# Weight subtractions in pieces of 240 and 256 columns, attention values loaded ahead of weights, and a few steps in another order

## The chip, the cores and the metric

The kernel runs on one core of a Trainium2 chip. The metric is the device time of one execution in microseconds (us), as the median of the runs. Before the change it is 815.58 us, over three runs of 815.52 to 818.22.

The engines are named as in the profile: PE is TensorE, PEld its weight loads, DVE is VectorE, ACT is ScalarE, POOL is GpSimd, SP issues DMAs.

## The reference

Two transformer-like layers on `x` of shape (16, 128, 256). The first mixes with a long convolution and a mixture of experts, the second with causal attention of 16 heads and a LoRA mixture of experts:

```python
x = x + tanh(g_xattn[0]) * L0_xattn(layernorm(x), k, fside_S2_0, ctx, ctx, 8)   # convolution stage
x = x + tanh(g_ffn[0])   * L0_ffn(layernorm(x), Wr, Wg, Wu, Wd, Sg, Su, Sd, Wsg)
x = x + tanh(g_xattn[1]) * mha(layernorm(x), ctx, ctx)                           # attention
x = x + tanh(g_ffn[1])   * L1_ffn(layernorm(x), gate_w, w_up, w_gate, w_down, ...)

def mha(q, k, v):                     # 16 heads of 16 columns, 128 queries, 128 keys
    scores = einsum("bhqd,bhkd->bhqk", qh, kh) / sqrt(hd)
    scores = where(causal, scores, -10000.0)
    return einsum("bhqk,bhkd->bhqd", softmax(scores), vh)
```

Everything is float32. Matrix products of the two feed-forward parts are made from a high and a low part of each operand: the high part is a copy in TensorE's rounded float32 (`fp32r`), the low part is the original minus the high part.

## The kernel before

The program is written by hand, engine by engine, with semaphores: each engine has one in-order list of instructions, and where it stands in the code is where it runs. The work is done for G = 4 groups of four batch rows. Its stages follow one another, with the first steps of each beside the last of the one before:

- The convolution stage, up to about 165 us. For each group and each of 16 head steps DVE multiplies (`a_kv`, L1168), PE convolves, DVE multiplies again (`a_z`, L1179), and POOL adds halves and quarters (`a_add`: L620 of 256 columns, L625 of 128). Between these adds, POOL makes the low parts of the shared experts' weights, `split_low` (L611): six tiles, five of 768 columns and one of 512. The first two come before the adds, the others behind adds 5 and 10 of groups 0 and 1 (`SPLITS`). DVE waits for POOL's add of the step before (`zh_ready`), POOL for DVE's product (`z_ready`).
- The experts, up to about 391 us, at whose end rows are scattered and then gathered back into `X` by DMAs that POOL issues (`gather`, L670, eight for each group).
- Attention, about 391 to 559 us, 32 steps: g is the group, k = 0 to 7 the half batch row in it. For a step, PE makes scores (`c_scores`: L2122, with the mask L2126), DVE takes the row maximum (L1551), bounds it (L1555) and subtracts it (L1561, all `c_shift`), ACT exponentiates (L910), PE turns the result (L2136, `c_turn_p`), ACT copies it out (L919, `c_evac`), PE multiplies with the values (L2147, `c_values`), ACT copies (L930, `c_take_ot`), PE turns back (L2160) and every second step DVE divides and adds to `X` (`c_finish`: L1569, L1570, L1575). The queries of later steps are normalised beside this, by small DVE instructions (`c_norm`: L1089 to L1121, taken a few at a time between the others through the object `Steps`) and an ACT instruction (L772, `c_norm_one`), and turned by PE (L2167).
- The last feed-forward part, from about 559 us to the end. Its weights are loaded and split during attention: SP loads a tile of 960 columns (`weights1`, L531), ACT copies the high part (L905, `c_high`) at k = 1 and 5, and POOL subtracts (L704, `split_low1`, 8 tiles). It stands behind all 32 gathers in POOL's list, in a loop.

SP's loop of attention loads, for each half group r, the keys of the next group (16 DMAs, L521), then a weight tile, which waits until POOL has done with the tile before it (`w1L_ready`), then the values of the next group (L525), which wait until PE has used the old ones (`pv_done`):

```python
sp.wait_ge(scores_ready, 8 * g + 4 * r + 4)
keys(g + 1, r)
weights1(g + 1, r)
sp.wait_ge(pv_done, 1 + 8 * g + 4 * r + 4)
values(g + 1, r)
```

Of the kernel before, what the change touches and what calls it, by code (L numbers as in the profile page):

```python
# [17 lines left out]
F32 = mybir.dt.float32  # L18
# [75 lines left out]
REGS_PER_LOAD = 20  # L94
XB = 12
AHEAD = 8
NORM_AT = (2, 0, 0)
NORMS_IN = {2: (4, 5), 3: (6, 7, 8), 4: (9, 10), 5: (11, 12), 6: (13, 14, 15)}
KBD_PIECES = 4
# [43 lines left out]
def flamingo_kernel(nc, x, ctx_nat, ctx_half, ctx_t, ctx_one, filt, bias, gates, w0, wr, w1, gw, ramp_in, out):  # L143
    es = ExitStack()
    with es:
# [280 lines left out]
        def _(sp):  # L426
# [101 lines left out]
            def weights1(g, r):  # L528
                if not isinstance(g, int) or g > 0:
                    sp.wait_ge(w1L_ready, 2 * g + r - 1)  # L530
                sp.dma_start(stg1[r], w1[bass.ds(2 * g + r, 1)].rearrange("a p n -> (a p) n")  # L531
                             ).then_inc(stg1_loaded[r], 16)
# [8 lines left out]
            with sp.Fori(0, G - 1) as g:  # L541
                for r in range(2):

                    sp.wait_ge(scores_ready, 8 * g + 4 * r + 4)
                    keys(g + 1, r)
                    weights1(g + 1, r)
                    sp.wait_ge(pv_done, 1 + 8 * g + 4 * r + 4)
                    values(g + 1, r)
            def rows(n):
                sp.wait_ge(rows_ready, n + 1)  # L550
                sp.dma_start(rows_d[n], prow).then_inc(rows_stored, 16)
                sp.wait_ge(rows_stored, 16 * (n + 1))
                if n >= 2:
                    sp.wait_ge(w_sum, n - 1)
                sp.dma_start(rb[n % 2], rows_d[n].rearrange("q t -> (q t)").partition_broadcast(P)
                             ).then_inc(rows_loaded, 16)
# [15 lines left out]
        def _(pool):  # L572
# [35 lines left out]
            def split_low(n):  # L608
                w = W0T if n < SJ - 1 else NSH - (SJ - 1) * W0T
                pool.wait_ge(wH_ready, n + 1)  # L610
                nc.gpsimd.tensor_tensor(sL[:, n * W0T:n * W0T + w], stg[:, n % 2, 0:w],  # L611
                                        sH[:, n * W0T:n * W0T + w].bitcast(F32), ALU.subtract).then_inc(wL_ready, 1)

            def a_add(g, h):

# [70 lines left out]
            for i in range(4):  # L686
                pool.wait_ge(y_stored[i], 16 * ((NBLK - 1 - i) // 4 + 1))
            pool.wait_ge(y_slots_ready, 2)
            for g in range(G):
                if g == PRE and PRE < G - 1:  # L690
                    zero_keys()
                pool.wait_ge(b_done, 1 + 2 * (g + 1))
                for i in (0, 2):
                    gather(g * BG + i, 0)
                    gather(g * BG + i + 1, 0)
                    for k in (i, i + 1):
                        pool.wait_ge(gathered[0][k], 16 * (g + 1))
                        gather(g * BG + k, 1)

            def split_low1(g, r):  # L700
                n = 2 * g + r
                pool.wait_ge(w1H_ready, n + 1)
                dst = bass.ds(n * W1C, W1C)
                nc.gpsimd.tensor_tensor(w1L[:, dst], stg1[r], w1H[:, dst].bitcast(F32), ALU.subtract  # L704
                                        ).then_inc(w1L_ready, 1)
            with pool.Fori(0, G) as g:
                for r in range(2):
                    split_low1(g, r)
            pool.wait_ge(w1L_ready, W1K)
# [14 lines left out]
        def _(act):  # L724
# [251 lines left out]
            for b in range(2):  # L976
                nc.scalar.activation(qT[:, b], bank[2][:, b * D:(b + 1) * D].rearrange("p (k t) -> p k t", k=DT),
                                     ACT.Copy).then_inc(qT_ready, 1)
            c_exp(0, 0)
            c_norm_one(0, 2)  # L980
            c_exp(0, 1)
            c_evac(0, 0)
            for g in range(G - 1):
                c_steps(g, True)
            c_steps(G - 1, False)
# [92 lines left out]
        def _(dve):  # L1078
# [763 lines left out]

            nc.vector.memset(OT, 0.0).then_inc(ot_zeroed, 1)
            c_shift(0, 0)
            rows_complete(0, 2, 4)
            c_norm(2, 4).take_all()
            c_shift(0, 1)
            c_shift(0, 2)
            for g in range(G - 1):
                c_steps(g, True)  # L1850
            c_steps(G - 1, False)
# [21 lines left out]
        def _(pe):  # L1873
# [313 lines left out]
            def c_steps(g, more):  # L2187
                for k in range(8):
                    turned = q_turned_in(g, k)
                    if turned:  # L2190
                        pe.wait_ge(ot_taken, 8 * g + k)
                        c_turn_q(*turned)
                    if not more and k in TURN_AT:
                        pe.wait_ge(ot_taken, 8 * g + k)
                        d_turn_x0(TURN_AT.index(k))
                    if k and (k < 6 or more):
                        c_scores(g + (k + 2) // 8, (k + 2) % 8)
                    if k:
                        c_turn_o(g, k - 1)
                    if turned:  # L2200
                        pe.wait_ge(qT_ready, BG * turned[0] + turned[1] + 1)
                    if not more and k in TURN_AT:
                        pe.wait_ge(x0T_ready, TURN_AT.index(k) + 1)
                    c_values(g, k)
                    if k < 7 or more:
                        c_turn_p(g + (k + 1) // 8, (k + 1) % 8)
                if more:
                    c_scores(g + 1, 2)
                c_turn_o(g, 7)
# [267 lines left out]
```

## Time and profile before

| | us |
|---|---|
| median of 3 runs (lowest, highest) | 815.58 (815.52, 818.22) |
| the profiled execution | 818.64 |
| its span, from the first instruction to the last | 816.9 |
| PE busy | 697.7 (85%) |
| DVE busy | 581.1 (71%) |
| ACT busy | 308.1 (38%) |
| POOL busy | 234.1 (29%) |

Mean granted TensorE clock over the span: 0.929, where 1 is 2.4 GHz and 0.5 is 1.2 GHz. In the chain that ended last PE has 56%, DVE 19% and POOL 6% of the span. A busy share is an average over stages with different limits; what matters is what is waited for in the stage in question. A row of a timeline reads: start, duration, engine, line, operation, output<-input, shape, count, and in brackets the idle time of the engine before it with what ended it. A DVE or POOL duration begins when the engine takes the instruction up, so time in which it cannot reach its operands is inside the duration.

### The profile page before, as it was taken

The page shows a single profiled execution, that of the slowest core. Times are in us where ns is not written, and L with a number is a line of the kernel's source. Part 1 is how long each engine was busy: PE and PEld are TensorE (multiplying, and loading weights), DVE is VectorE, ACT ScalarE, POOL GpSimd, SP SyncE. Part 2 cuts the span into 40 slices and gives each one's busy share as a digit, 9 for nine tenths or more (in the row PEclk, how much of TensorE's full clock was granted, in tenths as well). Part 3 has the DMA queues.
Part 4 walks back from the last instruction along what each step waited for, and adds up shares of the span by engine and source line. Part 5 has one row for each costly group of instructions (what it writes and reads, how often), then busy time and mean ns, then how long its engine had stood idle before and what let it go on. Part 6 is the DMA issues. An engine that isn't in the chain of part 4 may idle for free.

```text
span 816.9 us, 12649 instructions
## 1 busy us (share of the span) xinstructions
PE 697.7 (85%) x4198; PEld 563.6 (69%) x4214; DVE 581.1 (71%) x1234; ACT 308.1 (38%) x542; POOL 234.1 (29%) x246
## 2 busy tenths in 40 slices
PE   2878889889887799998787898877698999999994
PEld 1556667678776799987555565545587888888883
DVE  5888898675774466755679797874488768768664
ACT  2201101047632344423266575744344344343330
POOL 1888787710377000007675111101000000000000
PEclk9999999999999799999689796968799999999996
DMA  8202100033223344415553221100101001010000
GB/s 286 87 15 71 39 14 14 1 103 91 93 100 140 102 119 121 120 49 95 117 84 79 72 78 48 52 1 1 52 1 52 1 27 53 19 34 27 26 0 26
DMA packets 42925, 51.30 MB, mean 63 GB/s; under 512 B 7088, under 2 KB 36976, under 8 KB 42224
## 3 DMA queue, kind: packets, MB, share of 16 engines
q1 hardware_dynamic: 36720, 41.98, 16.5%
q0 software_dynamic: 6144, 8.52, 5.1%
q8 instruction: 36, 0.59, 0.3%
q14 instruction: 25, 0.20, 0.1%
HBM read 36.88 MB, written 13.59 MB: 62 GB/s over the span
## 4 chain that ended last, share of the span: by engine, by line
PE 56%; DVE 19%; issue 7%; POOL 6%; ACT 6%; SPq 4%; DMA 3%; DVEq 0%; POOLq 0%; ACTq 0%
PE bank L2216 22%; PE bank L2065 5%; PE bank L2085 4%; PE bank L2001 4%; PE bank L2136 3%; POOL A L620 2%; PE bank L2122 2%; DVE A L1561 2%; PE bank L2015 2%; DVE small L1551 2%; POOL A L625 2%; PE bank L1909 1%; POOL R L611 1%; PE bank L1921 1%; PE bank L2147 1%
## 5 line engine op out<-in xcount | busy, mean ns | idle before, releaser
L2216 PE MATMUL bank<-R 128*128 128x512 f32 (+3 forms) x1080 | 221.9, 366 | 21.5 <-DVE A L1684 6.1
L2216 PEld LDWEIGHTS bank<-R 128*128 128x128 f32 (+1 forms) x1080 | 183.5, 193 | 57.2 <-issue 7.3
L670 POOL DMA_INDIRECT X<-y_d,A x32 | 50.1, 1564 | 123.3 <-DMA y_d<-A 105.3
L2001 PE MATMUL bank<-R 128*128 128x512 f32 x264 | 67.4, 407 | 0.9 <-DVE R L1519 0.9
L620 POOL TENSOR_TENSOR A<-A 128x256 f32<-128x256 f32 x64 | 58.8, 918 | 7.6 <-DVE A L1179 7.5
L1909 PE MATMUL bank<-A 128*128 128x256 f32 x128 | 42.5, 414 | 19.8 <-DVE A L1168 7.1
L2001 PEld LDWEIGHTS bank<-R 128*128 128x128 f32 x264 | 50.4, 197 | 11.2 <-DVE R L1519 1.2
L1551 DVE TENSOR_REDUCE small<-bank 128x8 f32<-128x1024 f32 x32 | 38.9, 1217 | 26.1 <-PE bank L2126 26.0
L1179 DVE TENSOR_TENSOR A<-bank,A 128x512 f32<-128x512 f32 x64 | 43.8, 685 | 17.0 <-PE bank L1911 13.5
L720 POOL TENSOR_TENSOR A<-A 128x512 f32<-128x512 f32 x4 | 5.1, 1287 | 176.2 <-DVE A L1669 176.2
L1168 DVE TENSOR_TENSOR A<-A 128x512 f32<-128x512 f32 x64 | 53.0, 829 | 2.1 <-ACT A L746 2.1
L1700 DVE TENSOR_TENSOR A<-bank,A 128x512 f32<-128x512 f32 (+1 forms) x48 | 33.0, 688 | 28.0 <-PE bank L2216 27.6
L664 POOL DMA_INDIRECT x_d<-A x32 | 35.6, 1111 | 58.5 <-DVE A L1347 49.1
L2065 PE MATMUL bank<-R 128*128 x234 | 49.9, 351 | 0.7 <-DVE R L1507 0.7
L2015 PE MATMUL bank<-R 128*128 128x256 f32 (+1 forms) x288 | 42.2, 299 | 9.0 <-DVE R L1437 8.9
L2136 PE MATMUL bank<-ident,A 128*128 128x128 f32 x256 | 42.3, 319 | 7.5 <-ACT A L910 7.5
L1016 ACT ACTIVATE A<-bank 128x512 f32<-128x512 f32 (+1 forms) x48 | 28.6, 595 | 52.7 <-PE bank L2216 52.6
L2015 PEld LDWEIGHTS bank<-R 128*128 128x128 f32 (+1 forms) x288 | 39.5, 203 | 12.9 <-DVE R L1437 6.8
L704 POOL TENSOR_TENSOR R<-A,R 128x960 f32 x8 | 18.4, 2381 | 102.9 <-ACT R L905 102.9
L1909 PEld LDWEIGHTS bank<-A 128*128 128x128 f32 x128 | 20.6, 193 | 38.4 <-issue 37.5
L625 POOL TENSOR_TENSOR A<-A 128x128 f32<-128x128 f32 x64 | 42.8, 669 | 14.1 <-PE bank L1921 9.3
L2136 PEld LDWEIGHTS bank<-ident,A 128*128 128x128 f32 x256 | 33.7, 164 | 16.5 <-issue 8.6
(246 smaller groups left out, 1348.6 us busy)
## 6 DMA issues: line engine op xcount, KB each, us to landing
A<-x_d SPq DMA_DIRECT2D x39, 132.0 KB, 2.2
y_d<-A SPq DMA_DIRECT2D x39, 128.0 KB, 1.7
A<-rows_d SPq DMA_DIRECT2D x4, 1024.0 KB, 4.8
A<-in_w SPq DMA_DIRECT2D x8, 480.0 KB, 3.7
A<-in_w SPq DMA_DIRECT2D x5, 512.0 KB, 3.8
A<-in_ctx_one SPq DMA_DIRECT2D x8, 272.0 KB, 3.7
A<-in_ctx_half SPq DMA_DIRECT2D x8, 256.0 KB, 2.6
A<-in_ctx_nat SPq DMA_DIRECT2D x4, 512.0 KB, 3.9
```

The costliest lines, as they stand in the source:

```text
L620: nc.gpsimd.tensor_tensor(zh[:, u], zr[:, u, :, 0:HALF, :], zr[:, u, :, HALF:, :], ALU.add).then_inc(zh_ready, 1)
L625: nc.gpsimd.tensor_tensor(z2[:, :, :, h * I0:(h + 1) * I0], zh[:, u, :, 0:QUARTER, :], zh[:, u, :, QUARTER:, :], ALU.add).then_inc(z2_read ...
L670: nc.gpsimd.indirect_dma_start(out=X[:, b], out_offset=None, in_=y_d[:, :], in_offset=bass.IndirectOffsetOnAxis(ap=y_slots[:, b, r:r + 1], ...
L1168: nc.vector.tensor_tensor(kv[:, u], vT[:, :, t0:t0 + I0].unsqueeze(3).to_broadcast([P, 8, I0, I0]), c.unsqueeze(2).to_broadcast([P, 8, I0, ...
L1179: nc.vector.tensor_tensor(zr[:, u], yb[u].rearrange("p (q i j) -> p q i j", q=8, i=I0), c.unsqueeze(3).to_broadcast([P, 8, I0, I0]), ALU.m ...
L1551: step.mark(nc.vector.tensor_reduce(mx[:, u], S, AX_X, ALU.max))
L1909: nc.tensor.matmul(y[:, 0:n], diag, kv0, start=True, stop=False, skip_group_check=True)
L2001: mm = nc.tensor.matmul(dst, wX[:, a0:a0 + P], mX[:, k], start=(m == 0), stop=(m == 5))
L2015: mm = nc.tensor.matmul(DN[:, b * D:(b + 1) * D], hX[0:pr, n % 2, b * P:(b + 1) * P], wX[0:pr, a0:a0 + D], start=(j == 0 and m == 0 and b ...
L2065: mm = nc.tensor.matmul(GU[i % 2][:, 0:2 * EF], xX[:, i % 2, k * P:(k + 1) * P], w[:, k, :, :, bass.ds(expert[i] * RANK, RANK)], start=(m ...
L2136: mm = nc.tensor.transpose(PTP[:, h * P:(h + 1) * P], E_[:, k % 2, h], ident[:])
L2216: mm = nc.tensor.matmul(dst, a, m, start=start and n == 0, stop=stop and n == len(prods) - 1, skip_group_check=skip)
```

## The change

- `split_low` issues each subtraction as pieces of D = 256 columns (three, for the last tile two), `split_low1` as four pieces of W1Q = 240 columns. The semaphore is raised by the last piece.
- The first two of the eight `split_low1` no longer stand behind all gathers: the first stands ahead of the gathers of group 2, the second ahead of those of group 3. The loop over the rest is written out.
- SP's loop loads the values ahead of the weight tile.
- At the start of attention, DVE makes the second shift ahead of the normalisation of rows 2 and 3, and ACT copies out the first turned tile and makes the second exponential ahead of the normalised row.
- In the last group, PE makes scores (3, 6) and (3, 7) ahead of turning the rows of the next stage (`d_turn_x0`).

```diff
+W1Q = 240
@@ SP, the loop of attention
                     keys(g + 1, r)
-                    weights1(g + 1, r)
                     sp.wait_ge(pv_done, 1 + 8 * g + 4 * r + 4)
                     values(g + 1, r)
+                    weights1(g + 1, r)
@@ POOL, split_low
-                nc.gpsimd.tensor_tensor(sL[:, n * W0T:n * W0T + w], stg[:, n % 2, 0:w],
-                                        sH[:, n * W0T:n * W0T + w].bitcast(F32), ALU.subtract).then_inc(wL_ready, 1)
+                for q in range(0, w, D):
+                    at = n * W0T + q
+                    part = nc.gpsimd.tensor_tensor(sL[:, at:at + D], stg[:, n % 2, q:q + D],
+                                                   sH[:, at:at + D].bitcast(F32), ALU.subtract)
+                part.then_inc(wL_ready, 1)
@@ POOL, gathers and split_low1
+            def split_low1(g, r):
+                n = 2 * g + r
+                pool.wait_ge(w1H_ready, n + 1)
+                for q in range(0, W1C, W1Q):
+                    part = nc.gpsimd.tensor_tensor(w1L[:, n * W1C + q:n * W1C + q + W1Q], stg1[r][:, q:q + W1Q],
+                                                   w1H[:, n * W1C + q:n * W1C + q + W1Q].bitcast(F32), ALU.subtract)
+                part.then_inc(w1L_ready, 1)
+
             for g in range(G):
                 if g == PRE and PRE < G - 1:
                     zero_keys()
+                if g >= 2:
+                    split_low1(0, g - 2)
                 pool.wait_ge(b_done, 1 + 2 * (g + 1))
...
-            with pool.Fori(0, G) as g:
+            for g in range(1, G):
                 for r in range(2):
                     split_low1(g, r)
@@ ACT, start of attention
             c_exp(0, 0)
+            c_evac(0, 0)
+            c_exp(0, 1)
             c_norm_one(0, 2)
-            c_exp(0, 1)
-            c_evac(0, 0)
@@ DVE, start of attention
             c_shift(0, 0)
+            c_shift(0, 1)
             rows_complete(0, 2, 4)
-            c_norm(2, 4).take_all()
-            c_shift(0, 1)
-            c_shift(0, 2)
+            norm = c_norm(2, 4)
+            norm.take(4)
+            c_shift(0, 2, norm)
+            norm.take_all()
@@ PE, c_steps
+                    if k and (k < 6 or more):
+                        c_scores(g + (k + 2) // 8, (k + 2) % 8)
                     if not more and k in TURN_AT:
                         pe.wait_ge(ot_taken, 8 * g + k)
                         d_turn_x0(TURN_AT.index(k))
-                    if k and (k < 6 or more):
-                        c_scores(g + (k + 2) // 8, (k + 2) % 8)
```

Where instructions move, the lists read as follows. First ACT at the start of attention, before: A is the buffer of exponentials, turned tiles and rows, bank is PSUM, small the turned output.

```order
L910 ACTIVATE A<-A 128x1024 [waits shifted]
L772 ACTIVATE A<-X,A 128x256 [waits ln_ready]
L910 ACTIVATE A<-A 128x1024 [waits shifted]
L919 ACTIVATE A<-bank 128x1024 [waits p_turned]
L930 ACTIVATE small<-bank 128x256 [waits pv_done]
```

The same place after it, where the line numbers are those of the changed file (L918 is the exponential, L927 the copy of the turned tile, L780 the normalised row, L938 `c_take_ot`):

```order
L918 ACTIVATE A<-A 128x1024 [waits shifted]
L927 ACTIVATE A<-bank 128x1024 [waits p_turned]
L918 ACTIVATE A<-A 128x1024 [waits shifted]
L780 ACTIVATE A<-X,A 128x256 [waits ln_ready]
L938 ACTIVATE small<-bank 128x256 [waits pv_done]
```

The normalised row now stands directly ahead of `c_take_ot`, and behind the copy and the second exponential.

POOL's list after the change, at the gathers of group 2 (L674) and the first two subtractions in pieces (L697; A and y_d are the gather's slots and source, R the split weights):

```order
L674 DMA X<-y_d,A 128x256 [waits gathered0_3]
L697 TENSOR_TENSOR R<-A,R 128x240 [waits w1H_ready]
L697 TENSOR_TENSOR R<-A,R 128x240 x3
L674 DMA X<-y_d,A 128x256 [waits b_done]
L674 DMA X<-y_d,A 128x256
```

Before, every gather came first and the loop of subtractions behind them:

```order
L670 DMA X<-y_d,A 128x256 [waits gathered0_2]
L670 DMA X<-y_d,A 128x256 [waits gathered0_3]
L706 UNCONDITIONAL_BRANCH
L706 ISA
L704 ISA [waits w1H_ready]
L704 TENSOR_TENSOR R<-A,R 128x960
L702 REGISTER_ALU
L704 ISA [waits w1H_ready]
L704 TENSOR_TENSOR R<-A,R 128x960
```

So the gathers of groups 2 and 3 are now behind a wait for ACT's copy of a weight tile.

## Rows read from the trace of the kernel before

**Rows 1.** Stretches: us; busy PE, PEld, DVE, ACT, POOL; granted clock; DMA share, GB/s.

```profile
396.00:414.00 18.00, 13.22 (x76) 8.73 (x78) 11.35 (x29) 6.64 (x9) 11.17 (x8) 0.54 0.49 98
...
445.00:458.40 13.40, 12.02 (x65) 7.96 (x70) 8.04 (x20) 7.39 (x11) 0.40 (x1) 0.51 0.25 78
...
458.40:493.00 34.60, 30.55 (x320) 20.66 (x318) 32.08 (x66) 24.57 (x36) 4.74 (x3) 0.99 0.22 63
...
493.00:506.40 13.40, 11.73 (x70) 7.16 (x70) 8.83 (x19) 5.60 (x10) 1.54 (x1) 0.50 0.24 69
...
533.00:546.70 13.70, 9.21 (x59) 5.64 (x60) 9.39 (x23) 5.16 (x8) 0.00 (x0) 0.54 0.00 0
```

**Rows 2.** DVE's timeline at 437 us, and line 704 there.

```profile
437.52 4.45 DVE L1575 TENSOR_TENSOR X<-X,A 128x256 f32<-128x256 f32 x1
...
L704 POOL TENSOR_TENSOR R<-A,R x2: 2794/2804/2815, 436.7 to 438.9; 128x960 f32 x2
```

**Rows 3.** Timeline of SP, then PE, 411 to 444 us.

```profile
411.92 13.01 SPq L521 DMA_DIRECT2D A<-in_ctx_t  x16
...
439.68 0.35 SPq L531 DMA_DIRECT2D A<-in_w  x1
...
440.33 0.40 SPq L525 DMA_DIRECT2D A<-in_ctx_one  x1
...
443.87 0.65 PE L2147 MATMUL bank<-A 128*17 128x128 f32 x16 [2.00 <-DMA A<-in_ctx_one]
```

**Rows 4.** DVE's timeline, four maxima.

```profile
444.49 1.21 DVE L1551 TENSOR_REDUCE small<-bank 128x8 f32<-128x1024 f32 x1
...
457.82 1.23 DVE L1551 TENSOR_REDUCE small<-bank 128x8 f32<-128x1024 f32 x1 [3.32 <-PE bank L2126]
...
481.88 1.23 DVE L1551 TENSOR_REDUCE small<-bank 128x8 f32<-128x1024 f32 x1 [0.51 <-PE bank L2126]
...
489.89 1.22 DVE L1551 TENSOR_REDUCE small<-bank 128x8 f32<-128x1024 f32 x1
```

**Rows 5.** Lines 620, 1168: ns min/median/max, first and last start; then POOL's timeline.

```profile
L620 POOL TENSOR_TENSOR A<-A x64: 712/728/1700, 26.5 to 157.1; 128x256 f32<-128x256 f32 x64
...
L1168 DVE TENSOR_TENSOR A<-A x64: 650/683/1776, 17.3 to 153.5; 128x512 f32<-128x512 f32 x64
...
72.62 1.81 POOL L611 TENSOR_TENSOR R<-A,R 128x768 fp32r<-128x768 f32 x1
```

**Rows 6.** Start of attention: timeline of DVE, ACT and PE.

```profile
396.86 0.74 DVE L1089 BATCH_NORM_STATS2 A<-X 128x6 f32<-128x256 f32 x2
...
400.49 0.16 DVE L1121 SCALAR_TENSOR_TENSOR A<-A 128x2 f32<-128x2 f32 x1
...
403.17 1.21 DVE L1551 TENSOR_REDUCE small<-bank 128x8 f32<-128x1024 f32 x1
...
400.69 0.60 ACT L772 ACTIVATE A<-X,A 128x256 f32<-128x256 f32 x1 [2.66 <-DVE A L1121]
...
405.36 1.07 PE L2147 MATMUL bank<-A 128*17 128x128 f32 x16 [2.27 <-issue]
...
408.12 0.63 PE L2167 MATMUL bank<-ident,A 128*128 128x128 f32 x2
```

**Rows 7.** ACT's and POOL's timeline, 405 to 422 us.

```profile
417.26 0.99 ACT L905 ACTIVATE R<-A 128x960 fp32r<-128x960 f32 x1
...
405.91 1.54 POOL L670 DMA_INDIRECT X<-y_d,A  x1 [0.30 <-issue]
...
421.39 1.54 POOL L670 DMA_INDIRECT X<-y_d,A  x1 [0.30 <-issue]
```

**Rows 8.** DVE's timeline at two later subtractions.

```profile
459.08 1.17 DVE L1102 TENSOR_SCALAR A<-A 128x4 int32<-128x4 int32 x1
...
530.70 2.19 DVE L1114 TENSOR_TENSOR A<-A 128x4 f32<-128x4 f32 x1
```

**Rows 9.** PE's timeline in the last group.

```profile
541.05 0.66 PE L2173 MATMUL bank<-ident,A 128*128 128x128 f32 x2 [1.69 <-ACT A L941]
```

More of the change, by code:

```diff
@@ L698, in _ @@
                         gather(g * BG + k, 1)
[L700 to L705, printed above, removed]
-            with pool.Fori(0, G) as g:
+            for g in range(1, G):
                 for r in range(2):
```

## The prediction

> **What bounds the kernel now.** I read the stretches first, then the chain of waits, then the timelines of the places that the change touches. Attention runs from 391 to 559 us, some 168 us for 32 steps. The reader is to see in the stretches [rows 1] that PE is busy 88% of 458.4 to 493 at a granted clock of 0.99, and that the clock is at half (1.2 GHz, 0.50 to 0.54) in four stretches of 13 to 18 us. In three of them PE is as busy as elsewhere, so there PE's half speed is the bound; ahead of each PE had stood still for part of some us. At full speed DVE is as full as PE (32.1 against 30.6 of 34.6 us). So a stall of DVE can cost twice: by itself, and by the clock that falls behind it.
>
> The largest stall is at 437 us [rows 2]: DVE's addition to X (L1575), 0.42 us elsewhere, takes 4.45 us. POOL runs two subtractions of 960 columns there, 2.8 us each, from 436.7 to 441.7, and DVE is let in only at their end. Behind it PE waits another 2.0 us, to 443.87, for values that SP issued at 440.33, because they stood behind a weight tile that waited for POOL until 439.68; the keys ahead of both were out by 424.9 [rows 3]. Then the clock is at half.
>
> The rows for this say two things of the change. DVE waits for a whole POOL instruction, which speaks for short ones. But the second subtraction starts at 438.9, before the first has ended (436.7 + 2.8 = 439.5), and DVE does not get in between. The Trainium skill (GPSIMD Engine Reference, 2.1 Instruction dispatch) says that the cores of GpSimd begin their share of the next instruction without waiting for each other; the overlap of these two agrees, and by that rule adjoining pieces could hold DVE out as one long instruction. It is rival B below. In the convolution stage the same DVE operation never takes more than 1.78 us [rows 5] beside adjoining POOL instructions, so there it does get in.
>
> **The change, part by part.** Times are against the profiled execution, 818.64 us (span 816.9); that is 3.06 above the median of 815.58.
>
> 1. *Pieces of 256 in the convolution stage.* POOL's add of 256 columns takes 0.71 us undisturbed, a whole subtraction of 768 columns 1.81 [rows 5]. Three pieces with some 0.04 of overlap at each joint are 2.05, so +0.24 for each of five tiles, and about +0.1 for the one of two pieces: 1.3 us. POOL runs without a gap through most of groups 0 and 1 and DVE waits for its adds, so nothing hides it. DVE's L1168 (0.65 undisturbed, 1.78 at most, [rows 5]) would be held 1.1 us less for each tile: at best 6 × 1.1 = 6.6 less; at worst DVE comes in at one joint more of each tile, 6 × 0.65 = 3.9 more. It is POOL that is late, so I stay near its own row: **+1.3** (-2 to +4; all 6.6 would need POOL to have slack).
>
> 2. *Start of attention.* PE now gets its first turned tile at 401 instead of 405.3, as ACT no longer waits for the normalised row, and the 2.27 us of idle PE ahead of L2147 go [rows 6]. But the normalisation, 19 small steps from 396.86 to 400.65, is now broken up: 4 steps ahead of the third maximum, 4 beside it, 11 behind it. That maximum waits for scores and still starts at 403.17. Maximum, four small steps of 0.2 and subtraction are 3.2 us, to 406.4, and eleven steps of 0.2 end at 408.5. ACT's normalised row, 0.60 long and begun at 400.69 before, then ends at 409.2. `c_take_ot` stands behind it on ACT (0.4 us), and PE's turn of the query waits for both: 409.6 instead of 408.12 [rows 6], so +1.5. PE idles from about 406 to 409.6 at half clock, and the return to full clock may come later. Work at half clock costs double, so I add 0.4: **+1.9**. Bounds: -2.3 if nothing is late behind the idle time that goes, +4 if the clock returns some us later.
>
> 3. *First two subtractions ahead of gathers.* The first now follows ACT's copy (417.26 + 0.99, [rows 7], and about 2 later by part 2): 420.5 to 423, beside a normalisation on DVE. Up to one piece of 0.7 us is waited for at once: **+0.7**, bounds 0 and 2.7 (all four pieces). The gathers of group 2 follow, eight in 421.39 - 405.91 = 15.5 us [rows 7], so to 438.6 and landed by some 442.5. DVE wants them at about 448, so they are hidden by 5 us. Those of group 3 have 20 us and more.
>
> 4. *The pair at 437 us.* The two subtractions are now 16 us apart and in pieces. DVE's next maximum starts when the scores are there, at 441.7 instead of 444.49 [rows 4]; the values are in by 430, as they are issued right behind the keys. That is -2.8 on DVE, -3.2 on PE: **-3.0**. Without the values ahead of the weights, PE would still have stood until 443.8, and about 1.2 would be left; so of the 3.0 some 1.8 hang on that edit. Bounds: -0.5 if the pieces hold like one instruction, and -4.
>
> 5. *The clock behind it.* From 444.49 to 457.82 are two steps, 13.3 us at half clock; from 481.88 to 489.89 two steps with a normalisation too, 8.0 us at full clock [rows 4]. So 5.3 us if the fall at 445 goes. But full clock fell in the same part of the next group (493) and in the last (533) [rows 1], and not in that of group 0. I take half: **-2.7**, bounds 0 and -5.3.
>
> 6. *Later subtractions.* At 459.08 a small DVE step takes 1.17 instead of 0.17 us, at 530.70 one takes 2.19 instead of 0.16 [rows 8]. In pieces of 0.65 the first such step waits less. But it stands in a row of small steps 0.2 apart, and each of these finds the next piece: about as many waits as pieces, 0.5 each, sum 2. A gain is only there where a long DVE instruction on PSUM follows. **-0.3**, bounds -3 and +2.
>
> 7. *Scores ahead of turned rows.* PE's wait of 1.69 us for ACT's normalised row [rows 9] goes, as the scores stood behind it and need nothing of it. In the next step the exponential waits about 0.4 longer for ACT's copy: **-1.3**, bounds -2 and 0.
>
> Sum: 1.3 + 1.9 + 0.7 - 3.0 - 2.7 - 0.3 - 1.3 = -3.4, so 815.2 in that execution, and 812.2 as the median.
>
> A rule of the Trainium skill bears on parts 1 and 6 (SBUF — State Buffer, SBUF: two separate sides, on the port pair that DVE and GpSimd share): whoever starts first has the pair for the whole instruction. The 4.45 us agree in kind. By it alone a piece would bound every wait at 0.7 us, and part 6 would be -3.0 instead of -0.3.
>
> **The rivals.**
>
> A. *The clock stays up.* If stalls are shorter, the falls at 445 and at 493 or 533 may both go: 2.7 more in part 5, and for the other, of 0 to 5.3 by the same rows, I take 3.3. 812.2 - 2.7 - 3.3 = 806.2. For it: those stretches each follow a DVE stall on POOL. Against: at 493 the clock fell before the stall there could have slowed PE.
>
> B. *Pieces hold as one.* Parts 3 and 4 go to 2.7 and -1.5, part 6 to +0.7: 812.2 + 2.0 + 1.5 + 1.0 = 816.7. For it: the overlap in [rows 2]. Against: L1168's maximum [rows 5].
>
> C. *The start of attention costs and nothing is given back*, the case on the other side. The place is ACT's wait for the normalised row, ahead of `c_take_ot`. Part 2 goes to +4, and the later time shifts the steps so that the clock falls once more, in the one normalisation that ran at full clock (group 0, 415 to 431): +5.3, with part 5 at 0. 812.2 + 2.1 + 5.3 + 2.7 = 822.3. It decides once ACT's row ends later than about 409 and PE idles over 3 us there. For it: a fall behind PE's idle time at 396 [rows 1]. Against: stretches of a normalisation did pass at full clock.
>
> **How the numbers follow.** Forecast (809 to 816): 0.45. A: 0.25. B: 0.15. C: 0.15. A measurement of this kernel tells 0.5% from no change, which is 4.1 us: faster is below 811.5, slower above 819.7. The forecast's own range gives 0.19 faster and 0.26 same; A 0.23 and 0.02; B 0.01 and 0.11 with 0.03 slower; C 0.03 same and 0.12 slower. Together 0.43 faster, 0.42 same, 0.15 slower. The range for 8 in 10 takes in most of A, all of B and a part of C: 804 to 820.
>
> **What would show it.** Part 1: the last step of group 1 in the convolution stage about 1 us later, and DVE's L1168 never over 1.4. Part 2: PE's first turn of a query near 409.6 + 1.3, with over 3 us of idle PE ahead of it. Part 4: no L1575 over 1.2 us, no PE wait for values. Part 5: full clock through 445 to 458. Part 6: several DVE steps of 0.5 to 0.8 us in place of one of 2. Part 7: no PE wait for ACT's L941 ahead of scores. Wrong would be: an L1575 of 2 us or more (B), a DVE wait for gathered rows in group 1, or a new stretch at half clock between 415 and 437 (C).

## The result and the profile after

The changed kernel takes 806.62 us (805.19 to 815.86, 13 runs), the kernel before 818.22 beside it; the ratio is 0.988, 95% interval [0.9845, 0.9915]. In two later comparisons on other chips it was 0.991 [0.9874, 0.9946] and 0.9908 [0.9875, 0.9941]. So it is faster by about 1%, some 7 to 10 us, where 3.4 were forecast. The profiled execution of after took 805.39 us (span 803.6, mean granted clock 0.949), that of before 818.64 (816.9 and 0.929): 13.25 less. It is one of the changed kernel's quicker executions, so the ledger below, which is of this pair, adds up to more than the medians differ by.

The ledger goes by the starts of DVE's maxima (L1551 before, L1559 after), one for each of the 32 steps of attention; (g,k) is step k of group g. Eight of them as DVE's timeline of after has them (start us, duration us, then the operation and the idle time ahead):

```profile
394.11 1.16 DVE L1559 TENSOR_REDUCE small<-bank 128x8 f32<-128x1024 f32 x1
412.83 1.23 DVE L1559 TENSOR_REDUCE small<-bank 128x8 f32<-128x1024 f32 x1 [4.65 <-PE bank L2136]
435.10 1.22 DVE L1559 TENSOR_REDUCE small<-bank 128x8 f32<-128x1024 f32 x1 [0.73 <-PE bank L2136]
442.66 1.23 DVE L1559 TENSOR_REDUCE small<-bank 128x8 f32<-128x1024 f32 x1 [0.17 <-PE bank L2136]
450.79 1.22 DVE L1559 TENSOR_REDUCE small<-bank 128x8 f32<-128x1024 f32 x1
482.47 1.22 DVE L1559 TENSOR_REDUCE small<-bank 128x8 f32<-128x1024 f32 x1
498.59 1.22 DVE L1559 TENSOR_REDUCE small<-bank 128x8 f32<-128x1024 f32 x1
536.50 1.23 DVE L1559 TENSOR_REDUCE small<-bank 128x8 f32<-128x1024 f32 x1
```

| step | before | after | after less before | gained since the row above |
|---|---|---|---|---|
| (0,0) | 394.29 | 394.11 | -0.18 | -0.18 |
| (1,0) | 434.12 | 435.10 | +0.98 | +1.16 |
| (1,2) | 444.49 | 442.66 | -1.83 | -2.81 |
| (1,4) | 457.82 | 450.79 | -7.03 | -5.20 |
| (2,4) | 489.89 | 482.47 | -7.42 | -0.39 |
| (2,7) | 508.90 | 498.59 | -10.31 | -2.89 |
| (3,5) | 536.03 | 525.33 | -10.70 | -0.39 |
| (3,7) | 549.75 | 536.50 | -13.25 | -2.55 |

All of the difference has arisen by the last step of attention. The convolution stage gave nothing in the end, the start of attention cost 1.2 us, the place at 437 us gave 2.8, and the two steps behind it 5.2. The gain from (2,4) to (2,7) is not in every execution: another profile of the changed kernel (c2_after) takes 18.70 us for these three steps, where this one takes 16.12 and before takes 19.01.

The stretches say why these two steps shrank so much. First the stretches of [rows 1] in after, then after's own three at half clock in this part (busy PE, PEld, DVE, ACT, POOL; granted clock; DMA share, GB/s):

```profile
396.00:414.00 18.00, 12.35 (x71) 7.58 (x72) 10.08 (x27) 6.02 (x8) 4.53 (x3) 0.54 0.33 71
445.00:458.40 13.40, 11.54 (x116) 7.54 (x118) 12.84 (x37) 9.56 (x14) 8.79 (x6) 1.00 0.61 125
458.40:493.00 34.60, 29.23 (x288) 19.63 (x290) 31.22 (x62) 23.32 (x36) 8.77 (x13) 0.95 0.28 75
489.70:493.10 3.40, 3.40 (x28) 2.54 (x26) 2.58 (x4) 0.67 (x2) 0.00 (x0) 0.50 0.30 83
493.00:506.40 13.40, 12.73 (x125) 8.53 (x126) 10.24 (x15) 12.03 (x19) 2.30 (x4) 1.00 0.17 54
523.80:534.00 10.20, 8.85 (x58) 5.61 (x59) 8.29 (x22) 5.07 (x8) 0.00 (x0) 0.50 0.00 0
```

From 445 to 458.4 the clock was 0.51 before and is 1.00 now; PE issues 116 matmuls in place of 65 in about the same busy time. From 493 to 506.4, where it was 0.50, 3.4 us at half clock are left (489.7 to 493.1).

At 437 us the addition to X, 4.45 us in [rows 2], takes 0.87. DVE's timeline, then POOL's:

```profile
438.50 0.87 DVE L1583 TENSOR_TENSOR X<-X,A 128x256 f32<-128x256 f32 x1
439.29 1.21 DVE L1559 TENSOR_REDUCE small<-bank 128x8 f32<-128x1024 f32 x1
440.54 0.69 DVE L1563 TENSOR_SCALAR small<-small 128x8 f32<-128x8 f32 x1
...
436.74 1.54 POOL L674 DMA_INDIRECT X<-y_d,A  x1 [0.90 <-DMA X<-y_d,A]
437.73 3.46 POOL L697 TENSOR_TENSOR R<-A,R 128x240 fp32r<-128x240 f32 x4
```

SP's timeline answers to [rows 3]. The values (L526) and the weight tile (L532) are out by 426.7, ahead of the keys of 431, and nothing on SP waits for POOL. PE has no wait for a transfer in attention any more.

```profile
412.98 12.16 SPq L522 DMA_DIRECT2D A<-in_ctx_t  x16
425.43 0.41 SPq L526 DMA_DIRECT2D A<-in_ctx_one  x1
426.13 0.56 SPq L532 DMA_DIRECT2D A<-in_w  x1
431.11 11.95 SPq L522 DMA_DIRECT2D A<-in_ctx_t  x16
```

### The profile page after: what moved, and what is told of

Read it like the earlier page. It is cut to its first block, busy times and chain, and to the rows that moved or that the text cites. A ratio compares the mean times of both kernels' runs of the same rounds, so it can differ in the third digit from the quotient of the medians.

```text
span 803.6 us, 12659 instructions
## 1 busy us (share of the span) xinstructions
PE 685.7 (85%) x4198; PEld 555.2 (69%) x4214; DVE 575.7 (72%) x1234; ACT 307.8 (38%) x542; POOL 239.3 (30%) x281
## 4 chain that ended last, share of the span: by engine, by line
PE 55%; DVE 20%; issue 7%; POOL 6%; ACT 6%; SPq 4%; DMA 3%; DVEq 0%; POOLq 0%; ACTq 0%
PE bank L2226 23%; PE bank L2075 5%; PE bank L2095 4%; PE bank L2011 4%; DVE A L1569 2%; PE bank L2025 2%; POOL A L624 2%; PE bank L2146 2%; DVE small L1559 2%; PE bank L2132 2%; POOL R L614 2%; POOL A L629 2%; PE bank L1919 1%; PE bank L1931 1%; DVE A L1097 1%
## 5 line engine op out<-in xcount | busy, mean ns | idle before, releaser
L674 POOL DMA_INDIRECT X<-y_d,A x32 | 50.2, 1568 | 124.8 <-DMA y_d<-A 105.3
L624 POOL TENSOR_TENSOR A<-A 128x256 f32<-128x256 f32 x64 | 56.3, 880 | 7.6 <-DVE A L1187 7.5
L1176 DVE TENSOR_TENSOR A<-A 128x512 f32<-128x512 f32 x64 | 51.2, 801 | 2.1 <-ACT A L754 2.1
L1559 DVE TENSOR_REDUCE small<-bank 128x8 f32<-128x1024 f32 x32 | 38.9, 1216 | 17.4 <-PE bank L2136 17.3
L697 POOL TENSOR_TENSOR R<-A,R 128x240 fp32r<-128x240 f32 x32 | 22.9, 868 | 85.2 <-ACT R L913 85.2
L2146 PE MATMUL bank<-ident,A 128*128 128x128 f32 x256 | 38.9, 300 | 7.4 <-ACT A L918 7.2
L2146 PEld LDWEIGHTS bank<-ident,A 128*128 128x128 f32 x256 | 30.7, 153 | 15.9 <-issue 8.7
```

What stands on the lines that cost most here:

```text
L624: nc.gpsimd.tensor_tensor(zh[:, u], zr[:, u, :, 0:HALF, :], zr[:, u, :, HALF:, :], ALU.add).then_inc(zh_ready, 1)
L674: nc.gpsimd.indirect_dma_start(out=X[:, b], out_offset=None, in_=y_d[:, :], in_offset=bass.IndirectOffsetOnAxis(ap=y_slots[:, b, r:r + 1], ...
L1176: nc.vector.tensor_tensor(kv[:, u], vT[:, :, t0:t0 + I0].unsqueeze(3).to_broadcast([P, 8, I0, I0]), c.unsqueeze(2).to_broadcast([P, 8, I0, ...
L1559: step.mark(nc.vector.tensor_reduce(mx[:, u], S, AX_X, ALU.max))
L2146: mm = nc.tensor.transpose(PTP[:, h * P:(h + 1) * P], E_[:, k % 2, h], ident[:])
```

## The experiments

Each ran beside the kernel before. Steps are compared within profiles, totals by medians and intervals. There were three comparisons on three chips: one with e1 to e4, one with e5, e7, e8 and c_after, one with e6, e9, e10 and c2_after. The last two have the changed kernel itself as a control (812.75 and 810.54 us); the first has none, and there e4_weights_first (805.86 us), whose profile matches the changed kernel's, comes nearest to one. Line numbers of the runs differ from the changed kernel's by a few lines. Each fence of code shows the edit against the changed kernel, cut to the lines that change.

### Pieces taken back in attention (e3_attn_whole)

```
-W1Q = 240
+W1Q = 960
```

> The changed kernel with the eight subtractions of attention whole (960 columns), each still at its new place. Theory (the place pays, pieces hardly): the addition to X at 438 us waits up to 2 us once, the small DVE steps wait about as much in all; the total within 2 us of the changed kernel unless the clock falls once more (then 5 more). Rival (pieces are what pays): 5 us or more slower, with falls of the clock at 445 and 530 us as in the kernel before.

817.37 us (812.22 to 823.34), ratio 0.9987 [0.9956, 1.0018]: the whole gain is gone. Yet the place alone did repair 437 us: there the addition takes 0.97. The stall turned up 16 us later, at the second subtraction of the group (DVE's timeline and POOL's, then the stretch behind it):

```profile
458.58 3.33 DVE L1122 TENSOR_TENSOR A<-A 128x4 f32<-128x4 f32 x1
...
458.10 1.54 POOL L674 DMA_INDIRECT X<-y_d,A  x1 [0.30 <-issue]
459.07 2.81 POOL L697 TENSOR_TENSOR R<-A,R 128x960 fp32r<-128x960 f32 x1
```

```profile
458.40:472.00 13.60, 11.68 (x72) 6.85 (x69) 10.42 (x18) 4.42 (x7) 3.48 (x2) 0.51 0.37 87
```

A step on 4 columns, 0.16 us elsewhere, takes 3.33: it began inside the gather and ended with the subtraction (459.07 + 2.81 = 461.88). Then the clock is at 0.51. So moving whole subtractions moves the stall and the fall of the clock with it. From (1,4) to (2,0), the four steps around this stall, this kernel takes 22.51 us and the changed one 16.10. The theory that the place pays and the pieces hardly do fell.

### Place taken back, pieces kept (e5_pair)

```
-                if g >= 2:
-                    split_low1(0, g - 2)
...
-            for g in range(1, G):
+            for g in range(G):
```

> The changed kernel with all eight subtractions of attention behind the gathers again, but in pieces of 240. Theory (pieces alone take most of the stall, as DVE gets in between two of them; the place is secondary): eight pieces in a row near 437 us, the addition to X waits at most 1.2 us, the weight tile comes late but the values do not wait for it; the total within 2 us of the changed kernel. Rival (the place pays): DVE's steps beside eight pieces wait several us in all, the clock falls at 445 us, the total 5 us or more higher.

816.46 us (from 812.03; one of its 12 executions took 3652 us and weighs nothing in a median), ratio 0.9955 [0.9928, 0.9983]. DVE's timeline, then SP's, then PE's:

```profile
443.22 2.17 DVE L1581 TENSOR_TENSOR X<-X,A 128x256 f32<-128x256 f32 x1
...
431.30 0.41 SPq L526 DMA_DIRECT2D A<-in_ctx_one  x1
443.24 0.35 SPq L532 DMA_DIRECT2D A<-in_w  x1
443.85 12.19 SPq L522 DMA_DIRECT2D A<-in_ctx_t  x16
...
457.51 2.08 PE L2130 MATMUL bank<-A 32*128 32x256 f32 x8 [3.64 <-issue]
```

Here the eight pieces stand in a row behind the last gather, which runs from 438.86 to 440.40 (POOL's timeline):

```profile
439.85 6.07 POOL L697 TENSOR_TENSOR R<-A,R 128x240 fp32r<-128x240 f32 x8
```

The addition takes 2.17 us, half of [rows 2]: it is held over more than one piece, but let in at 445.39, before the last of them ends (445.92). From (1,0) to (1,2) it is 8.18 us, against 10.37 before and 7.56 in after, so at this place pieces alone bring most of the gain. But the weight tile still waits for POOL until 443.24, and now the next keys stand behind it: they go out at 443.85 instead of 431.11, the last is issued at 456.04, PE stands still for 3.64 us until 457.51, ahead of the first scores that use them, and step (1,4) starts 7.95 us behind (1,3) instead of 3.27. (The profile names no releaser for this wait; that it is the keys follows from SP's order and these times.) With values ahead of weights the hold has moved from the values to the keys. So in this order of SP's loads, pieces without the place are worth little, and both are needed. Pieces alone with the old order of the loads were not tried; there the values would again stand behind the late weight tile, as in [rows 3].

### Halves (e9_halves)

```
-W1Q = 240
+W1Q = 480
```

> The changed kernel with pieces of 480 columns in attention (1.35 us each) instead of 240. If DVE waits for at most the piece that is running, the addition to X at 437 to 441 takes at most some 1.8 us (0.42 + 1.35), the clock stays up behind it, and the total is 0 to 2 us above the changed kernel's. If the size must be small because adjoining pieces hold DVE out together, the addition or the subtraction beside them takes 2.5 us or more, the clock falls at about 455, and the total is 5 us or more above.

815.33 us (812.62 to 820.19), ratio 0.9967 [0.994, 0.9994], against 0.9908 for quarters beside it and 0.9987 for wholes in another comparison. The additions to X were never over 1.12 us, as the theory of the single piece has it. But at 458 us:

```profile
458.13 3.33 DVE L1124 SCALAR_TENSOR_TENSOR A<-A 128x4 f32<-128x4 f32 x1
...
457.51 1.54 POOL L674 DMA_INDIRECT X<-y_d,A  x1 [0.30 <-issue]
458.50 2.93 POOL L697 TENSOR_TENSOR R<-A,R 128x480 fp32r<-128x480 f32 x2
```

DVE's step began while the gather was open, 0.37 us ahead of the listed start of the subtraction, and was let go at the end of the second half (461.46 against 461.43): a hold as long as that of one whole. The gather alone does not hold such a step: in after one takes 0.16 at 456.91, inside the gather of 455.46 to 457.15. The clock was 0.75 from 458.4 to 472. Away from gathers there was no such long hold. The same small step behind the maximum of (0,4) meets the first subtraction in all three sizes (DVE's timelines of after, of halves, of wholes):

```profile
418.97 0.65 DVE L1563 TENSOR_SCALAR small<-small 128x8 f32<-128x8 f32 x1
```

```profile
420.56 1.17 DVE L1563 TENSOR_SCALAR small<-small 128x8 f32<-128x8 f32 x1
```

```profile
421.21 2.18 DVE L1563 TENSOR_SCALAR small<-small 128x8 f32<-128x8 f32 x1
```

0.65, 1.17, 2.18 for pieces of 0.69, 1.20, 2.22 us: there the wait is at most the piece that runs. The difference between the two places is in POOL's durations (ns min/median/max of L697, in after and in the kernel with wholes):

```profile
L697 POOL TENSOR_TENSOR R<-A,R x32: 684/695/1522, 418.9 to 544.9; 128x240 fp32r<-128x240 f32 x32
```

```profile
L697 POOL TENSOR_TENSOR R<-A,R x8: 2209/2220/2807, 421.1 to 556.0; 128x960 fp32r<-128x960 f32 x8
```

Behind a gather a subtraction starts 0.55 us before the gather is over (457.51 + 1.54 = 459.05 against 458.50) and is listed some 0.6 us longer, 2.81 for 2.22. Pieces behind it overlap by as much: there is no moment between them at which POOL has nothing open. The pair of the kernel before stood in the same way behind its last gather, which is open until 437.26 while the first subtraction is listed from 436.70 (POOL's timeline of before; for the pair see [rows 2]):

```profile
435.72 1.54 POOL L670 DMA_INDIRECT X<-y_d,A  x1 [0.88 <-DMA X<-y_d,A]
```

This overlap as the cause of the long holds is argued from the times, not shown by an experiment: no kernel kept a subtraction away from every gather. A skew between POOL's cores would fit what the Trainium skill says (Perfetto Trace Analysis, DMA Instruction — SWDGE (GPSIMD)): two of them write a gather's descriptors. No row here shows single cores.

### The changed kernel again (c2_after, c_after)

> The changed kernel itself, for comparison in this call: 805 to 813 us as in its earlier runs, ratio 0.985 to 0.994.

810.54 us, ratio 0.9908. Its profiled execution took 812.46, 7.1 more than that of after, and shows where one program's executions part. At (1,4) they are 0.23 us apart (451.02 against 450.79); then, behind the gathers (DVE, then the stretch):

```profile
457.57 1.74 DVE L1124 SCALAR_TENSOR_TENSOR A<-A 128x4 f32<-128x4 f32 x1
```

```profile
458.40:472.00 13.60, 11.29 (x86) 7.17 (x86) 9.32 (x18) 6.49 (x10) 0.89 (x2) 0.75 0.22 68
```

In after, DVE met the same four pieces with 0.37 and 0.62 (458.80 and 459.20) and the clock stayed up. By (2,0) the two are 4.9 us apart, and another 2.6 come between (2,5) and (2,7), where the clock is 0.62 from 493 to 506.4. So even quarters hold DVE together now and then when they overlap; its addition at 438.71 took 1.67 as well, over the 1.2 us that the prediction set as its mark. A hold of 1.7 need not cost that: e6_old_tail below had one of 1.73 at 460.7 and no fall before 494.9. What decides whether a hold is followed by a fall is not shown.

The other control:

> The changed kernel itself, as the mark for the other kernels of this call. Both theories: 805 to 808 us in most runs, 811 to 816 in some, and the same order of events as in its first profile.

812.75 us (804.85 to 816.35); its profiled execution (804.85) is after's within 0.5 us at nearly every maximum.

### Weights ahead of values (e4_weights_first)

```
                     keys(g + 1, r)
+                    weights1(g + 1, r)
...
                     values(g + 1, r)
-                    weights1(g + 1, r)
```

> The changed kernel with SP loading the weight tile ahead of the values again. Theory: POOL frees the tile at about 421 us, ahead of the end of the keys' issues, so the wait for it is short now and the values come only about 0.5 us later: no wait of PE for values, same total. Rival (the order of the loads is what pays): PE waits 2 us for values near 440 us and the total is 2 us or more higher.

805.86 us (805.1 to 813.73), ratio 0.9864 [0.9819, 0.9909], maxima equal to after's within 0.25 us. SP's timeline:

```profile
425.67 0.44 SPq L532 DMA_DIRECT2D A<-in_w  x1
426.40 0.40 SPq L526 DMA_DIRECT2D A<-in_ctx_one  x1
```

The tile's slot is free by then, because the first subtraction now comes ahead of the gathers. Beside the new place of the subtractions, the order of the loads is worth nothing.

### The tail's old order (e6_old_tail)

```
-                    if k and (k < 6 or more):
-                        c_scores(g + (k + 2) // 8, (k + 2) % 8)
                     if not more and k in TURN_AT:
                         pe.wait_ge(ot_taken, 8 * g + k)
                         d_turn_x0(TURN_AT.index(k))
+                    if k and (k < 6 or more):
+                        c_scores(g + (k + 2) // 8, (k + 2) % 8)
```

> The changed kernel with PE's turned rows again ahead of its scores in the last group; all else as changed. If part 7 of the prediction is right, PE again stands still some 1.7 us ahead of L2177's turned rows for ACT's normalised row, and the maxima of steps (3,6) and (3,7) come 1.3 to 2.3 us later than 531.67 and 536.50, so the total is 1.3 to 2.3 us above the changed kernel's of the same call. If the order of the tail is worth nothing because PE is at half clock there anyway or ACT's exponentials bound the steps, those maxima stay within 0.5 us and the total within 0.5.

813.15 us (808.57 to 818.97), ratio 0.9931 [0.9897, 0.9965]; 2.6 above the control, with intervals that overlap. The profile is clear: PE's wait is back, and (3,6) starts 8.69 us behind (3,5), as before, instead of 6.34 (PE, then DVE's two maxima):

```profile
535.31 0.66 PE L2183 MATMUL bank<-ident,A 128*128 128x128 f32 x2 [1.69 <-ACT A L949]
...
530.29 1.22 DVE L1559 TENSOR_REDUCE small<-bank 128x8 f32<-128x1024 f32 x1
538.98 1.22 DVE L1559 TENSOR_REDUCE small<-bank 128x8 f32<-128x1024 f32 x1 [4.03 <-PE bank L2136]
```

So the edit is worth 2.35 us in the profile: the wait of 1.69 and the turn itself, 0.66, which also stood ahead of the scores.

### The convolution stage's pieces taken back (e1_conv_whole)

```
-                for q in range(0, w, D):
+                for q in range(0, w, w):
```

(and slices of `w` for those of `D`)

> The changed kernel with the subtractions of the convolution stage whole again (768 columns). Theory (pieces there cost POOL time, about 0.24 us each tile): DVE's additions to X at the ends of groups 0 and 1 come 1.1 and 1.3 us earlier than in the changed kernel (at 65.9 and 101.7 us), the total 0 to 1.3 us lower if nothing later takes it back. Rival (pieces let DVE in and pay there): these additions come later than in the changed kernel, the total higher. Rival (the 1.3 us are given back by TensorE's clock behind 158 us): same total, with the half-clock stretch at 158.5 us back.

808.01 us (805.77 to 818.49), ratio 0.9854 [0.9814, 0.9894]: no worse than the changed kernel. The additions at the ends of groups 0 and 1 were expected at 65.9 and 101.7; they came at 67.93 and 103.78. This execution had already lost time early, with the clock at 0.79 from 26 to 34 us, where it is at 1.00 in after, so its profile can't be compared with after's by absolute times. From the one addition to the other it takes 35.85 us, before 35.84 and after 36.04.

In after, groups 0 to 2 end later than before: their last additions (L1202 before, L1210 after) are at 66.99, 103.03 and 136.49 against 65.85, 101.69 and 135.16, so +1.14, +1.34, +1.33. But the fourth is at 162.22 against 162.37. The stretch from 157 to 162 us, of before and of after:

```profile
157.00:162.00 5.00, 3.21 (x15) 3.21 (x16) 2.25 (x4) 0.00 (x0) 3.41 (x4) 0.66 0.02 5
```

```profile
157.00:162.00 5.00, 2.21 (x18) 1.87 (x17) 3.17 (x6) 0.00 (x0) 4.66 (x6) 1.00 0.02 5
```

Before, a part of it was at half clock; after, none. That gives the 1.3 us back. A kernel with whole subtractions in a quick execution (e10_best_again, below) confirms it: its additions are at 65.56, 101.42, 134.88 and 162.12, and its stretch is that of before:

```profile
157.00:162.00 5.00, 3.48 (x17) 3.49 (x18) 2.01 (x3) 0.00 (x0) 3.13 (x3) 0.66 0.02 5
```

That the clock would give it back is not something I could have read from before.

### The start of attention (e2_old_start, e7_mixed_start)

The first has the old order on both engines. The second has DVE's old order, and on ACT only the evacuation ahead:

```
             c_exp(0, 0)
             c_evac(0, 0)
-            c_exp(0, 1)
             c_norm_one(0, 2)
+            c_exp(0, 1)
...
             c_shift(0, 0)
-            c_shift(0, 1)
             rows_complete(0, 2, 4)
-            norm = c_norm(2, 4)
-            norm.take(4)
-            c_shift(0, 2, norm)
-            norm.take_all()
+            c_norm(2, 4).take_all()
+            c_shift(0, 1)
+            c_shift(0, 2)
```

> The changed kernel with the old order at the start of attention on DVE and ACT. Theory (the new order there costs, as the query's turn waits for the normalised row): PE's first turn of a query at 408.1 instead of 409.1 us, the maximum of step (0,3) about 1 us earlier, the total 0 to 1.5 us lower. Rival (the new start pays): the total 1 us or more higher.

> The changed kernel with DVE's old order at the start of attention (normalisation ahead of the second shift) and ACT copying the first turned tile ahead of the normalised row, then the second exponential. Theory (the start costs because DVE's normalisation ends late): the normalised row is ready at 401.3 us, PE's first turn of a query moves from 409.1 to about 406.5, the maximum of step (0,3) from 18.7 us behind that of step (0,0) to about 16; the total 1 to 3 us lower unless the clock's falls move. Rival (PE at half clock is the bound there, whatever the order): no change at step (0,3).

From (0,0) to (0,3) it is 17.48 us before, 18.72 after, 17.52 with the old start and 15.67 with the mixed one. The totals don't follow: 811.04 (ratio 0.9912 [0.9878, 0.9946]) and 810.79 (0.9881 [0.985, 0.9912]). In the mixed one's profile the clock was at half again at 465 us and for 10 us from 492.6, and what the start had saved was gone by (2,7): from (0,0) to there it takes 107.77 us, the changed kernel 104.48. So by itself the start shows in its own steps and not in the total.

### The best version (e8_best, e10_best_again)

The mixed start, and whole subtractions in the convolution stage.

> As the kernel with the mixed start, and the subtractions of the convolution stage whole. Theory: both gains, 1 to 3 us at the start of attention and 1.3 us in the convolution stage, so 2 to 4 us below the changed kernel if the clock's falls stay where they are. Rival (the clock decides): the total anywhere within 5 us of the changed kernel, following the mean granted clock.

> The same kernel as e8_best (convolution subtractions whole, DVE's old order at the start of attention, ACT: both first exponential and evacuation ahead of the normalised row, the second exponential behind it), beside the changed kernel in one call. If it is the better version, its ratio to before is again below 0.987 and its fastest runs lie 2 us or more below the changed kernel's (804 to 805). If the first result was luck of the clock, the two agree within 1 us in their fastest runs.

805.69 us (800.89 to 812.54), ratio 0.9844 [0.9797, 0.9891], and 806.55 (801.55 to 812.9), ratio 0.9878 [0.9833, 0.9924]; the second misses the expected 0.987 by a little. The changed kernel beside them: 812.75 and 810.54. Each pair of intervals overlaps. Taken together, the median of its 12 executions is 806.2, that of the changed kernel's 16 is 812.3, and five of the 12 lie below the lowest of the 16 (804.85). None of the changed kernel's 13 executions in the first comparison lies below 804.85 either, but their median is 806.62. So the quickest executions speak for this version; that its median is lower is not settled. DVE's third and fourth maxima show the start: the third comes at once (in after it stands behind 2.71 us of idle DVE), and the fourth comes 15.54 us behind the first (at 395.92 in this execution).

```profile
404.83 1.21 DVE L1559 TENSOR_REDUCE small<-bank 128x8 f32<-128x1024 f32 x1
411.46 1.23 DVE L1559 TENSOR_REDUCE small<-bank 128x8 f32<-128x1024 f32 x1 [3.95 <-PE bank L2134]
```

## Why the prediction was right and where it was not

The direction, the largest place and the terms 2, 4 and 6 held; the forecast of 812.2 us was 5.6 above the 806.6 measured, within its range. The gain was two to three times the 3.4 forecast. That the later medians of the changed kernel, 812.75 and 810.54, lie so near 812.2 is luck: the kernel before ran at 818.95 and 818.89 beside them, some 3.3 us above the 815.58 from which the forecast was taken.

One reading was wrong from the start. PE is not as busy as elsewhere in three of the four stretches at half clock [rows 1] but in two, 90% and 88%; in the other two it is 73% and 67%. So half speed bounds the two at 445 and 493, and the other two less.

1. *Convolution stage, +1.3.* The first three groups end 1.1 to 1.3 us later, and DVE's L1176 is never over 1.21 us, as said. What was missed is that the delay is given back at 157 to 162 us by the clock. Net -0.2.
2. *Start of attention, +1.9.* +1.16 by (1,0), +1.24 by (0,3). PE's turn of the query starts at 409.13 (409.6 forecast), behind 3.26 us of idle PE:

```profile
409.13 0.69 PE L2177 MATMUL bank<-ident,A 128*128 128x128 f32 x2 [3.26 <-ACT small L938]
...
408.21 0.60 ACT L780 ACTIVATE A<-X,A 128x256 f32<-128x256 f32 x1 [6.20 <-DVE A L1129]
408.71 0.36 ACT L938 ACTIVATE small<-bank 128x256 f32<-128x256 f32 x1
```

   The mechanism is the one named: the row on ACT waits 6.2 us for DVE's broken-up normalisation. ACT's small copy runs beside the row's end, which I had put behind it; that is the half microsecond. The 0.4 for the clock did not come. The order without that flaw is the mixed start, which is 3.05 us quicker to (0,3).
3. *First subtraction ahead of gathers, +0.7.* One small step waits 0.65, as said, but on DVE it costs the path nothing: (0,5) is +1.06, (1,0) +0.98. Gathers start 0.3 us later than before [rows 7] and nothing waits for them.
4. *The pair at 437, -3.0.* -2.81. Right in size. Wrong is that 1.8 of it hang on the values being loaded first: without that edit the step is the same (e4_weights_first). I had let the weight tile wait for POOL until 439.68 as before, though the subtraction it waits for had itself moved ahead of the gathers.
5. *The clock behind it, -2.7.* This is the term that was mis-sized. The whole 5.3 of its own working came (-5.20), and in all three profiles of the changed kernel the clock is at 1.00 from 445 to 458.4. Halving the term on the ground that the clock also falls at the same part of the next group was wrong: the fall at 445 went all the same. The fall at 493 shrank too in this pair, another -2.89, but not in every execution: from (2,4) to (2,7) after and c_after take 16.12 us, c2_after 18.70, before 19.01. Why it shrinks in some is not shown.
6. *Later subtractions, -0.3.* Small, as said (-0.39 from (1,4) to (2,4), and again from (2,7) to (3,5)), and the reason given is seen. DVE's row of small steps at 485 us meets one piece after the other:

```profile
485.62 0.49 DVE L1124 SCALAR_TENSOR_TENSOR A<-A 128x4 f32<-128x4 f32 x1
486.15 0.62 DVE L1119 SCALAR_TENSOR_TENSOR A<-A 128x4 f32<-128x4 f32 x1
486.81 0.61 DVE L1122 TENSOR_TENSOR A<-A 128x4 f32<-128x4 f32 x1
```

   1.24 of extra wait in three parts, where one subtraction of 2.2 us had cost 1.0 and 2.0 [rows 8]. The -3.0 that would follow from one bounded wait per subtraction (Trainium skill, SBUF — State Buffer, SBUF: two separate sides) did not come, since each step begins a wait of its own. What I left out is the subtraction that now stands behind gathers at 458 us. In pieces of 240 it costs little in after, and 1.6 and the clock in c2_after; whole or halved it costs 3.2 and the clock.
7. *Scores ahead of turned rows, -1.3.* -2.35, shown by e6_old_tail. I took the wait less the exponential's delay; the turn itself, 0.66, goes too. The exponential does come later, 7.05 us behind the maximum of (3,5) instead of 6.00, but PE has other work until it is there and doesn't wait for it.

Rival A (the clock stays up) is close to what happened: of its two falls the one at 445 went, and the one at 493 shrank to 3.4 us. It had 0.25. But its 806.2 is in part a coincidence with 806.6: it has nothing of what came back in parts 1, 2, 3 and 7, and its 3.3 us for the second fall are not in every execution. Rival B (pieces hold as one) is wrong for pieces on their own and in part right for pieces behind a gather: over two halves a DVE step takes 3.33 us, over eight quarters 2.17, which is not to their end, over four 0.62 to 1.74. The overlap in [rows 2], which spoke for it, was the sign of this. Rival C fell: part 2 stayed under +1.9, and in after no new stretch at half clock came between 415 and 437.

The sum of the ledger is -13.25 and that of my terms -3.4. Of the difference of 9.85, 5.4 is the clock in part 5, 1.5 part 1, 0.7 each parts 2 and 3, and 1.05 part 7; the rest is small.

What stays open: why executions reach attention up to 6 us apart. The first maximum is at 393.9 to 394.4 in before, after, c_after, c2_after, e4_weights_first and e10_best_again, and at 395.7 to 400.3 in the eight others. The profiles part early: the clock from 26 to 34 us is 1.00 in the first six and 0.79 to 0.86 in the other eight, whichever pieces they have. What makes it fall there is not shown. Absolute times in attention are therefore compared only within the first six; for the others the document goes by differences between steps. A piece size below 240 and a subtraction that never follows a gather were not tried.

## What to carry to other kernels

Before cutting a POOL instruction short for DVE's sake, look at what runs on POOL just before it. Here a piece bounded DVE's wait only where the pieces didn't follow an indirect DMA; behind one they overlapped, and held DVE for several. Put the work elsewhere, or cut it finer there. Price a stall at its own length plus the stretch at half clock that stands behind it in the profile, at full value, and look at more than one execution: a hold of 1.7 us had a fall behind it in c2_after and none in e6_old_tail. And when an order is changed in two places, ask of each edit whether the other has already taken its wait away.

## What the runs showed of the hardware

- A POOL subtraction directly behind a gather is listed as starting 0.55 to 0.57 us before the gather's end, and as about 0.6 us longer: 2.81 for 2.22 us (960 columns), 1.28 to 1.52 for 0.69 (240).
- A DVE step on 4 columns with two inputs in SBUF, begun during a gather with a subtraction behind it, was released only at the end of the subtraction, 3.33 us later, both for one whole (e3_attn_whole) and for two halves (e9_halves).
- The clock had been at half for 13.4 us behind one PE wait of 2.0 us [rows 1, 3], and was at 1.00 in that stretch when the wait and the hold of 4.45 us ahead of it were gone.
